# A lambda layer behind a group norm: key maximum on TensorE, group statistics on GpSimd, twelve image buffers, two pairs as plain sums

## The chip, the core and the metric

The kernel runs on one core of a Trainium2 chip. The core has five engines that run beside each other and are joined by semaphores: TensorE (PE, matmuls into PSUM), VectorE (DVE), ScalarE (ACT), GpSimd (POOL) and SyncE (SP, which here issues all transfers). The metric is the time of one execution on the device, in microseconds (us); the median of three runs of the kernel before is 1595.41 us (1594.87 to 1595.89).

## The reference

Cut to what is computed (b = 32 images, d = 128 channels, n = m = 1024 positions, k = 16, h = 4 heads, v = 32):

```
xg = group_norm(x, 32 groups of 4 channels)          # per image
xf = xg.reshape(b, n, d)                              # 1024 rows of 128
keys    = xf @ Wk.T          ; softmax over the 1024 positions
values  = batch_norm(xf @ Wv.T)                       # per position, over images and v
queries = batch_norm(xf @ Wq.T)                       # per k, over everything else
content_lambda   = einsum('bmk,bmv->bkv', softmax_keys, values)
position_lambdas = einsum('nmk,bmv->bnkv', E, values) # E is (1024, 1024, 16): the large product
out = x + einsum('bknh,bkv->bhvn', queries, content_lambda)
        + einsum('bknh,bnkv->bhvn', queries, position_lambdas)
```

## The kernel before

All is float32. A large product is made of two roundings: a matrix is split by ScalarE into a high part (type fp32r, `e_hi`, `v_hi`) and by VectorE into what is left (`e_lo`, `b_lo`, `t_lo`), and three matmuls (hi by hi, lo by hi, hi by lo) are summed.

**Projection stage.** The 32 images come one by one into eight buffers `x_in` (4 KB for each of 128 partitions), in nine batches: two of 2 images, seven of 4. For a batch VectorE takes `BN_STATS` of each half image and combines them (`gn_moments`), TensorE averages over the groups of 4 partitions (`gn_average`), VectorE and ScalarE make scale and shift (`gn_finish`, `gn_sqrt`, a square root on ScalarE), and GpSimd normalises the images in place (`norm_images`, L398). TensorE then transposes an image (L909, 8 matmuls) and projects the one before it (L919), and ScalarE reads both out of PSUM, into `x_t`, and into `v_nat`, `keys`, `q_nat`. After eight images (an octave `a`, four in all) the softmax's maximum is made: VectorE takes it within a partition (`keys_max`), and GpSimd over the partitions by `partition_all_reduce` and subtracts it (`shift_keys`, L403 and L405). `between` says behind which batch VectorE does the statistics of an octave.

**Stage between.** VectorE makes the values' statistics, both engines normalise the values, TensorE makes the content lambdas (64 matmuls, L950) and their sums; differences of value blocks (`t_raw`) are made and everything is split in two parts.

**The pairs.** E is read in 64 pairs of two tiles of 8 rows. With its two halves of positions and the two halves of the images a pair is a 2 by 2 block product. It is made by seven products (`product`, i = 0 to 6, L989) of 4 x 3 matmuls of 128x512, with sums of E's blocks made by GpSimd (`e_sums`, `e_last_sum`) and differences of the values' blocks; banks a, b and c of PSUM are read out between the products by VectorE into `pos` (`evacuate_...`). The pair's lambdas are then multiplied by the queries (`query`, 32 matmuls, L1008), which stands behind product 0 of the next pair; GpSimd spreads the queries for it over `q_diag` (`diag`), and VectorE adds the result to the image (`add_out`).

Every engine runs its list in the order that is written out by hand, so an instruction that waits holds all behind it.

## Time and profile before

| what | value |
|---|---|
| median of three runs | 1595.41 us |
| the profiled execution's own time | 1599.93 us |
| its span (first to last instruction) | 1598.2 us |
| mean TensorE clock granted | 0.968 of full |
| TensorE busy (matmul) | 1483.3 us, 93% |
| VectorE busy | 1016.7 us, 64% |
| GpSimd busy | 675.6 us, 42% |
| ScalarE busy | 427.5 us, 27% |

The slices of the span show where TensorE isn't busy: the first six of forty read 6, 7, 6, 5, 3, 6 tenths, the last 7, and all 33 between them 8 or 9. A busy share says nothing of a wait that comes once; the stretch before the even part is read by stage.

### The profile page before, as it was taken

To read this page: it belongs to the slowest core of one execution; us is meant where nothing else is said; L and a number is where in the kernel's file an instruction comes from. 1 tells how busy PE (TensorE), PEld (TensorE's weight loads), DVE (VectorE), ACT (ScalarE), POOL (GpSimd) and SP (SyncE) were. 2 spreads that over 40 slices of the span, in tenths; PEclk is the share of its full clock that TensorE was granted. 3 is DMA by queue.
4 is the path that set the end of the run, shared out by engine and by line. 5 is a ranking of instruction groups with operands and counts; after the bars stand their busy time and mean duration, and the time that the engine had idled before them with its cause. 6 is when DMAs were issued, how large, how long until landed. Compare 5 with 4: busy or idle time off the path is not lost.

```text
span 1598.2 us, 27819 instructions
## 1 busy us (share of the span) xinstructions
PE 1483.3 (93%) x10407; PEld 1243.3 (78%) x10407; DVE 1016.7 (64%) x1496; ACT 427.5 (27%) x738; POOL 675.6 (42%) x453
## 2 busy tenths in 40 slices
PE   6765368999999999999999999999999999999997
PEld 6655247888888888888888888888888888888886
DVE  6645597666666666666666666666666666666663
ACT  4435432222222222222222222222222222222220
POOL 4333525444444444444444444444444444444441
PEclk9878689999999999999999999999999999999999
DMA  6453142233343434241525243333434251525221
GB/s 227 170 192 112 15 65 60 60 90 68 74 85 85 85 85 86 60 92 45 112 59 112 59 103 67 78 67 85 85 85 85 76 95 47 92 58 112 59 52 27
DMA packets 338460, 134.68 MB, mean 84 GB/s; under 512 B 202640, under 2 KB 333824, under 8 KB 337920
## 3 DMA queue, kind: packets, MB, share of 16 engines
q1 hardware_dynamic: 338432, 134.31, 36.7%
q8 instruction: 17, 0.28, 0.1%
q14 instruction: 11, 0.09, 0.0%
HBM read 109.12 MB, written 25.17 MB: 84 GB/s over the span
## 4 chain that ended last, share of the span: by engine, by line
PE 87%; issue 5%; DVE 3%; POOL 3%; ACT 1%; DMA 0%; DVEq 0%; SPq 0%; POOLq 0%; ACTq 0%
PE ps_a L989 76%; PE ps_b L1008 8%; PE ps_b L919 2%; POOL x_in L398 1%; PE ps_a L909 1%; POOL keys L405 1%; DVE e_lo L679 1%; POOL key_top L403 0%; DVE b_lo L691 0%; DVE bn L639 0%; PE ps_b L950 0%; DVE q_stats L671 0%; DMA x_in<-in_x 0%; DVE t_lo L691 0%; ACT x_t L500 0%
## 5 line engine op out<-in xcount | busy, mean ns | idle before, releaser
L989 PE MATMUL ps_a<-v_hi,e_hi 128*128 128x512 f32 x1792 | 706.0, 394 | 12.8 <-issue 12.1
L989 PE MATMUL ps_a<-v_hi,e_lo 128*128 128x512 f32 x1792 | 699.0, 390 | 0.0
L989 PEld LDWEIGHTS ps_a<-v_hi,e_hi 128*128 128x128 f32 x1792 | 337.1, 188 | 86.6 <-issue 12.9
L989 PE MATMUL ps_a<-b_lo,e_hi 128*128 128x512 f32 x1024 | 399.2, 390 | 2.6 <-DVE b_lo L691 2.6
L989 PEld LDWEIGHTS ps_a<-v_hi,e_lo 128*128 128x128 f32 x1792 | 337.3, 188 | 68.2
L525 ACT ACTIVATE e_hi<-e_nat 128x512 fp32r<-128x512 f32 x320 | 202.1, 632 | 603.4 <-PE ps_a L989 598.3
L437 POOL TENSOR_TENSOR q_diag<-qn,row_mask 128x1024 f32<-128x1024 f32 x128 | 249.1, 1967 | 222.4 <-PE ps_b L1008 208.2
L433 POOL TENSOR_TENSOR e_nat<-e_nat,s_buf 128x512 f32<-128x512 f32 x64 | 83.5, 1305 | 553.3 <-DVE e_lo L679 553.3
L679 DVE TENSOR_TENSOR e_lo<-e_nat,e_hi 128x512 fp32r<-128x512 f32 x320 | 301.1, 941 | 2.0 <-ACT e_hi L525 0.3
L989 PE MATMUL ps_a<-t_lo,e_hi 128*128 128x512 f32 x768 | 300.0, 391 | 0.0
L752 DVE TENSOR_TENSOR pos<-ps_a,content 128x512 f32<-128x512 f32 x189 | 130.7, 692 | 178.4 <-PE ps_a L989 175.9
L989 PEld LDWEIGHTS ps_a<-b_lo,e_hi 128*128 128x128 f32 x1024 | 192.5, 188 | 43.4 <-DVE b_lo L691 3.5
L790 DVE TENSOR_TENSOR res<-ps_b,res 32x512 f32 (+1 forms) x256 | 175.9, 687 | 57.7 <-PE ps_b L1008 55.0
L525 ACT ACTIVATE e_hi<-s_buf 128x512 fp32r<-128x512 f32 x128 | 80.8, 633 | 401.4 <-PE ps_a L989 401.4
L679 DVE TENSOR_TENSOR e_lo<-s_buf,e_hi 128x512 fp32r<-128x512 f32 x128 | 105.2, 822 | 109.7 <-ACT e_hi L525 109.5
L989 PEld LDWEIGHTS ps_a<-t_lo,e_hi 128*128 128x128 f32 x768 | 144.6, 188 | 30.4
L1008 PEld LDWEIGHTS ps_b<-q_diag,pos 128*64 128x64 f32 x4096 | 126.2, 139 | 29.7 <-issue 28.5
L1008 PE MATMUL ps_b<-q_diag,pos 128*64 128x64 f32 x4096 | 135.1, 225 | 7.1 <-DVE pos L854 6.3
L424 POOL TENSOR_TENSOR s_buf<-s_buf,e_nat 128x512 f32<-128x512 f32 x64 | 103.8, 1621 | 5.0
L422 POOL TENSOR_TENSOR s_buf<-e_nat 128x512 f32<-128x512 f32 x64 | 84.0, 1313 | 0.0
L426 POOL TENSOR_TENSOR e_nat<-e_nat 128x512 f32<-128x512 f32 x64 | 83.9, 1310 | 0.0
L779 DVE TENSOR_TENSOR pos<-ps_a,pos 128x512 f32<-128x512 f32 x64 | 44.3, 691 | 54.7 <-PE ps_a L989 54.7
(107 smaller groups left out, 758.5 us busy)
## 6 DMA issues: line engine op xcount, KB each, us to landing
e_nat<-in_L_conv_E SPq DMA_DIRECT2D x128, 512.0 KB, 4.8
x_in<-in_x SPq DMA_DIRECT2D x32, 512.0 KB, 4.2
res<-in_x SPq DMA_DIRECT2D x64, 256.0 KB, 6.8
out_dram<-res SPq DMA_DIRECT2D x64, 256.0 KB, 4.9
q_dram<-q_nat SPq DMA_DIRECT2D x4, 2048.0 KB, 7.6
q_blk<-q_dram SPq DMA_DIRECT2D x32, 256.0 KB, 5.4
gam_q<-in_L_conv_gamma_q SPq DMA_DIRECT2D x8, 0.1 KB, 4.9
bet_q<-in_L_conv_beta_q SPq DMA_DIRECT2D x8, 0.1 KB, 4.6
```

The source lines that it names most:

```text
L422: pool.tensor_tensor(s_buf[:, 0], e_block(slot, 1, 0), e_block(slot, 1, 1), ALU.add).then_inc(s_ready, 1)
L424: pool.tensor_tensor(s_buf[:, 1], s_buf[:, 0], e_block(slot, 0, 0), ALU.subtract).then_inc(s_ready, 1)
L426: pool.tensor_tensor(a21, e_block(slot, 0, 0), a21, ALU.subtract).then_inc(s_ready, 1)
L433: pool.tensor_tensor(a12, a12, s_buf[:, 1], ALU.subtract).then_inc(s_ready, 1)
L437: pool.tensor_tensor(q_diag[:, slot].rearrange("p (q n) -> p q n", n=TN), qn[:, slot].unsqueeze(2).to_broadcast([P, BH, TN]), row_mask[:]. ...
L525: nc.scalar.activation(e_hi[:, i], e_source(i, slot), ACT.Copy).then_inc(e_hi_ready, 1)
L679: nc.vector.tensor_tensor(e_lo[:, i], e_source(i, slot), e_hi[:, i].bitcast(f32), ALU.subtract).then_inc(e_lo_ready, 1)
L752: nc.vector.tensor_tensor(to, bank_a, content[:, cols], ALU.add).then_inc(evacuated, 1)
L779: nc.vector.tensor_tensor(pos[:, 0, right], bank_b, pos[:, 0, right], ALU.add).then_inc(evacuated, 1)
L790: ins = nc.vector.tensor_tensor(r, s, r, ALU.add)
L989: ins = nc.tensor.matmul(BANK_OF[i], e[:, i, j].rearrange("p n k -> p (n k)"), v[:, j], start=(STARTS[i] and j == 0 and n == 0), stop=(STO ...
L1008: ins = nc.tensor.matmul(to, pos[:, t, cols], q_diag[:, t, cols], start=True, stop=True)
```

## The change

1. **Key maximum.** `partition_all_reduce` goes. TensorE transposes `key_max` (`turn_key_max`), VectorE takes the maximum along the free dimension and scales a unit matrix by it (`keys_top`), TensorE multiplies by a matrix of ones, which spreads it to all partitions (`spread_key_top`), VectorE copies it to SBUF (`copy_key_top`), GpSimd subtracts. For the last octave VectorE subtracts, out of PSUM. These use the PSUM columns of one projection buffer, so TensorE's next projection waits for the copy.
2. **Group statistics.** VectorE no longer combines the statistics: the raw sets are squared by one operation, averaged by TensorE, copied, and nine small operations on GpSimd, each waiting for the one before, make scale and shift; the inverse root is `pow` with -0.5 on GpSimd, here and for the values and the queries. ScalarE has no more square roots.
3. **Twelve buffers** for the images instead of eight; `gn_average` of a batch stands one image earlier in each four, and VectorE takes a batch's raw statistics ahead of the octave's work.
4. **Two pairs as plain sums.** Pairs 0 and 1 need no block sums: eight block products (96 matmuls a pair instead of 84) into four banks, with the hi parts straight from ScalarE. Those of pair 0's first half of positions stand ahead of the content lambdas. Their reading out adds `content` at once. What GpSimd did between (`v_nat` difference) VectorE does now.

The core of the diff:

```
-            def gn_sqrt(k):
-                act.wait_ge(gn_var_ready, k + 1)
-                nc.scalar.activation(gn_std[:, slots(k)], gn_var[:, slots(k)], ACT.Sqrt, bias=eps_t[:]).then_inc(gn_std_ready, 1)
             def norm_images(k):
-                pool.wait_ge(gn_ready, k + 1)
+                pool.wait_ge(gn_read, k + 1)
+                link(pool.tensor_tensor(gn_half[:, sl], gn_out[:, sl, 0], gn_out[:, sl, 1], ALU.add))
...
+                link(pool.tensor_tensor(gn_rstd[:, sl], gn_var[:, sl], minus_half[:, sl], ALU.pow))
+                link(pool.tensor_tensor(gn_bias[:, sl], gn_tot[:, sl, 1], gn_rstd[:, sl], ALU.mult))
+                link(pool.tensor_scalar(gn_bias[:, sl], gn_bias[:, sl], -1.0, 0.0, ALU.mult, ALU.add))
             def shift_keys(a):
-                pool.wait_ge(key_max_ready, a + 1)
-                link(pool.partition_all_reduce(key_top[:].rearrange("p g k -> p (g k)"),
-                                               key_max[:].rearrange("p g k -> p (g k)"), P, RMAX))
+                pool.wait_ge(key_spread_ready, a + 1)
+            def turn_key_max(a, reads):
+                pe.wait_ge(key_max_ready, a + 1)
+                pe.wait_ge(proj_read, reads)
+                nc.tensor.transpose(turned_ps, key_max[:].rearrange("p g k -> p (g k)"), ident[:]).then_inc(key_max_turned, 1)
+            def spread_key_top(a):
+                pe.wait_ge(ones_ready, 1)
+                pe.wait_ge(key_diag_ready, a + 1)
+                nc.tensor.matmul(spread_ps, ones_sq[:], key_diag[:], start=True, stop=True).then_inc(key_top_spread, 1)
+            def plain_sums(p, j, passes, last=False):
+                half, slots_of = j // MJ, FIRST_SLOTS[p]
+                for at, (tile, col, bank) in enumerate(((1, 1, bank_d), (1, 0, bank_c), (0, 0, bank_a), (0, 1, bank_b))):
...
+                    if p == 1 and j == 0:
+                        pe.wait_ge(evacuated, (4, 5, 6, 7)[at])
+                    for n, (e, v) in enumerate(((e_hi, hi), (e_lo, hi), (e_hi, lo))):
+                        if n in passes:
+                            ins = nc.tensor.matmul(bank, e[:, slot, j % MJ].rearrange("p n k -> p (n k)"), v,
+...
+            for j in range(MJ):
+                pe.wait_ge(v_hi_ready, j + 1)
+                plain_sums(0, j, (0, 1))
+            lambda_half(0)
+            lambda_half(1)
+            sum_lambdas()
...
+            for j in range(MJ, J - 1):
+                plain_sums(1, j, (0, 1, 2))
+            query(0, first=True)
+            plain_sums(1, J - 1, (0, 1, 2), last=True)
```

Not shown: the same `pow` in `values_rstd` and `queries_rstd`, and what follows from pairs 0 and 1 being plain in the lists of the engines.

On GpSimd, at the batch of images 12 to 15 and the first octave's maximum, before (`key_top` is the reduced maximum, `keys` the projected keys):

```order
L398 TENSOR_SCALAR x_in<-x_in,gn_rstd,gn_bias 128x1024 [waits gn_ready]
L398 TENSOR_SCALAR x_in<-x_in,gn_rstd,gn_bias 128x1024 x3
L403 ISA
L403 ISA key_top<-key_max 128x128 [waits key_max_ready]
L405 ISA
L405 TENSOR_TENSOR keys<-keys,key_top 128x64x16 [waits pool_step]
```

and now, one batch later:

```order
L418 TENSOR_TENSOR gn_half<-gn_out 128x24 [waits gn_read]
L419 TENSOR_TENSOR gn_tot<-gn_half 128x12 [waits pool_step]
L420 TENSOR_TENSOR gn_sq<-gn_tot 128x4 [waits pool_step]
L421 TENSOR_SCALAR gn_var<-gn_tot 128x4 [waits pool_step]
L422 TENSOR_TENSOR gn_var<-gn_var,gn_tot 128x4 [waits pool_step]
L423 TENSOR_TENSOR gn_var<-gn_var,gn_sq 128x4 [waits pool_step]
L424 TENSOR_TENSOR gn_rstd<-gn_var,minus_half 128x4 [waits pool_step]
L425 TENSOR_TENSOR gn_bias<-gn_tot,gn_rstd 128x4 [waits pool_step]
L426 TENSOR_SCALAR gn_bias<-gn_bias 128x4 [waits pool_step]
L429 TENSOR_SCALAR x_main<-x_main,gn_rstd,gn_bias 128x1024 [waits pool_step]
L429 TENSOR_SCALAR x_main<-x_main,gn_rstd,gn_bias 128x1024 x3
L434 TENSOR_TENSOR keys<-keys,key_spread 128x64x16 [waits key_spread_ready]
```

The reduce and the ISA instructions around it are gone, and nine small operations stand ahead of each batch's images.

On TensorE, from the last projection on, before:

```order
L919 MATMUL ps_b<-w_cols,x_t 128x112 x16
L950 MATMUL ps_b<-v_nat,keys 64x128 x64
L957 MATMUL ps_a<-ones,exp_sum 128x1 x4
L989 MATMUL ps_a<-v_hi,e_hi 128x512
L989 MATMUL ps_a<-v_hi,e_lo 128x512
```

and now (with the waits; of the 32 matmuls of L1080 the first two stand):

```order
L996 MATMUL ps_b<-ident,key_max 128x128 [waits proj_read,key_max_ready]
L1001 MATMUL ps_b<-key_diag,ones_sq 128x128 [waits key_diag_ready,ones_ready]
L1080 MATMUL ps_a<-v_hi,e_hi 128x512 [waits v_hi_ready,e_lo_ready]
L1080 MATMUL ps_a<-v_hi,e_lo 128x512
...
L1037 MATMUL ps_b<-v_nat,keys 64x128 [waits v_normed,keys_exp]
```

Thirty-two matmuls of pair 0 moved ahead of the content lambdas.

On VectorE, among the products of pair 0 (`t_lo`, `b_lo` lo parts of the values' differences, `q_stats` the queries' statistics, `pos` and `head` the lambdas, `res` the output), before:

```order
L746 COPY head<-ps_a 128x512 [waits product_done]
L679 TENSOR_TENSOR e_lo<-e_nat,e_hi 128x512 [waits e_hi_ready]
L691 TENSOR_TENSOR b_lo<-v_nat,v_hi 128x4x512 [waits v_hi_ready]
L754 COPY pos<-ps_a 128x512 [waits product_done]
...
L691 TENSOR_TENSOR b_lo<-v_nat,v_hi 128x4x512 [waits lam_half,v_hi_ready]
L679 TENSOR_TENSOR e_lo<-e_nat,e_hi 128x512 [waits e_hi_ready]
L691 TENSOR_TENSOR t_lo<-t_raw,v_hi 128x2048 [waits v_hi_ready]
```

and now, from the first evacuations of pair 0 to its query result:

```order
L805 TENSOR_TENSOR pos<-ps_a,content 128x512 [waits first_summed] x3
...
L720 TENSOR_TENSOR t_lo<-t_raw,v_hi 128x2048 [waits t_hi_ready]
L720 TENSOR_TENSOR b_lo<-v_nat,v_hi 128x4x512 [waits t_hi_ready]
L720 TENSOR_TENSOR t_lo<-t_raw,v_hi 128x2048 [waits t_hi_ready]
L705 TENSOR_TENSOR e_lo<-e_nat,e_hi 128x512 [waits e_hi_ready]
L705 TENSOR_TENSOR e_lo<-s_buf,e_hi 128x512 [waits e_hi_ready] x2
L805 TENSOR_TENSOR pos<-ps_a,content 128x512 [waits queried,first_summed]
L805 TENSOR_TENSOR pos<-ps_a,content 128x512 [waits first_summed] x3
L705 TENSOR_TENSOR e_lo<-e_nat,e_hi 128x512 [waits e_hi_ready] x3
L817 TENSOR_TENSOR res<-ps_b,res 32x32x16 [waits queried,res_loaded]
```

The lo parts of the differences, which before stood between the products of pair 0 (L691), now stand behind the queries' statistics, ahead of pair 2's first splits and of `res`.

## Rows read from the trace of the kernel before

**Rows 1.** Stages: length, busy PE, PEld, DVE, ACT, POOL, PE's clock, DMA share, GB/s.
```profile
11.28:146.20 134.92, 101.73 (x784) 98.78 (x784) 79.39 (x227) 68.20 (x136) 50.96 (x41) 0.86 0.47 163
146.20:269.33 123.13, 61.85 (x393) 50.43 (x393) 86.55 (x139) 40.06 (x49) 51.91 (x31) 0.76 0.29 58
269.33:1598.20 1328.87, 1318.79 (x9229) 1093.39 (x9228) 844.61 (x1113) 317.15 (x549) 569.05 (x365) 1.00 0.36 77
```
**Rows 2.** Chain that ended last: start, us, what; two of the even pairs.
```profile
356.53 19.27 PE ps_a L989 x84
377.81 19.27 PE ps_a L989 x84
```
**Rows 3.** Waits before 269 us: who waited for what, us in total, times, longest.
```profile
POOL keys L405 <- issue: 32.6, 4, 10.3
POOL key_top L403 <- issue: 26.8, 4, 7.8
PE ps_a L909 <- POOL x_in L398: 25.2, 7, 11.8
```
**Rows 4.** TensorE in order of time: start, length, instruction, idle before it.
```profile
26.45 1.04 PE L909 MATMUL ps_a<-ident,x_in 128*128 128x128 f32 x8
27.33 1.94 PE L919 MATMUL ps_b<-w_cols,x_t 128*128 128x112 f32 x16
...
39.84 2.04 PE L919 MATMUL ps_b<-w_cols,x_t 128*128 128x112 f32 x16 [1.17 <-ACT x_t L500]
...
142.44 3.72 PE L919 MATMUL ps_b<-w_cols,x_t 128*128 128x112 f32 x32
...
185.25 8.88 PE L950 MATMUL ps_b<-v_nat,keys 128*64 128x128 f32 x128 [39.09 <-ACT keys L515]
...
246.34 3.69 PE L1008 MATMUL ps_b<-q_diag,pos 128*64 128x64 f32 x64 [6.28 <-DVE pos L854]
...
269.33 2.08 PE L1008 MATMUL ps_b<-q_diag,pos 128*64 128x64 f32 x64
```
**Rows 5.** GpSimd in order of time.
```profile
1.20 0.10 POOL L379 MEMSET eps_t<- 128x1 f32 x1
46.30 5.44 POOL L398 TENSOR_SCALAR x_in<-x_in,gn_rstd,gn_bias 128x1024 f32<-128x1024 f32 x4 [7.88 <-DVE gn_bias L658]
...
139.93 0.46 POOL L415 TENSOR_TENSOR exp_sum<-level 128x128 f32<-128x128 f32 x1
140.35 1.27 POOL L422 TENSOR_TENSOR s_buf<-e_nat 128x512 f32<-128x512 f32 x1
...
190.78 6.69 POOL L461 TENSOR_TENSOR v_nat<-v_nat 128x2048 f32<-128x2048 f32 x1 [0.47 <-issue]
234.51 4.32 POOL L437 TENSOR_TENSOR q_diag<-qn,row_mask 128x1024 f32<-128x1024 f32 x2 [14.18 <-ACT qn L590]
```
**Rows 6.** The line of the reduce: queue's instructions, count, ns.
```profile
L403 POOLq MODIFY_POOL_CONFIG  x8: 8/11/22, 51.7 to 164.0; - x8
```
**Rows 7.** VectorE in order of time.
```profile
33.50 4.84 DVE L639 BATCH_NORM_STATS2 bn<-x_in 128x6 f32<-128x512 f32 x8
59.24 5.31 DVE L671 BATCH_NORM_STATS2 q_stats<-q_nat 128x6 f32<-128x256 f32 x16
164.64 4.43 DVE L723 TENSOR_SCALAR v_nat<-v_nat,v_scale,v_shift 128x1024 f32<-128x1024 f32 x6
192.96 6.66 DVE L735 TENSOR_TENSOR t_raw<-v_nat,t_raw 128x2048 f32<-128x2048 f32 x1
200.14 2.28 DVE L691 TENSOR_TENSOR t_lo<-t_raw,v_hi 128x2048 fp32r<-128x2048 f32 x1
205.35 3.02 DVE L803 SCALAR_TENSOR_TENSOR lam_diag<-ps_b,inv_sum,row_mask 64x128 f32<-64x128 f32 x8
226.57 2.08 DVE L812 BATCH_NORM_AGGREGATE q_mv<-q_stats 128x2 f32<-128x24 f32 x16
235.31 1.70 DVE L679 TENSOR_TENSOR e_lo<-e_nat,e_hi 128x512 fp32r<-128x512 f32 x1 [0.26 <-ACT e_hi L525]
```

More of the change, by code:

```diff
@@ new lines, in _ @@
+            first_lo(0, 3)
+            for j in range(MJ):
+                dve.wait_ge(v_hi_ready, j + 1)
+                nc.vector.tensor_scalar(v_nat[:, j], v_nat[:, j], v_scale[:, j:j + 1], v_shift[:, j:j + 1],
+                                        ALU.mult, ALU.add).then_inc(v_normed, 1)
+            dve.wait_ge(v_normed, MJ)
+            link(nc.vector.tensor_tensor(t_raw[:, 0], raw_block(v_nat, 0, 1), raw_block(v_nat, 0, 0), ALU.subtract))
+            some_query_stats(2, range(4, KD)).then_inc(q_stats_done, 1)
@@ L847, in _ @@
-            evacuate_c21(0, with_content=False)
-            for n in range(NP - 1):
-                split_lo(1, n, 1)
-            evacuate_c12(0)
-            dve.wait_ge(content_ready, 1)
-            dve.wait_ge(evacuated, NP)
-            for t in range(2):
-                nc.vector.tensor_tensor(pos[:, t], pos[:, t], content[:], ALU.add).then_inc(content_added, 1)
+            t_split_lo(2, 2)
+            t_split_lo(3, 3)
+            t_split_lo(5, 4)
+            split_lo(2, 0, 0)
+            split_lo(2, 1, 0)
@@ L856, in pair @@
+            split_lo(2, 2, 0)
+            evacuate_first(1)
+            for n in range(3, NP - 1):
+                split_lo(2, n, 0)
+            add_out(0, new_block=True)
             def pair(p, i, second, last):
@@ L877, in pair @@
                     split_lo(p + 1, 5, (i + 1) % 2)
-            for i in range(1, PPB):
-                pair(i, i, i == 1, False)
+            for i in range(2, PPB):
+                pair(i, i, i == 2, False)
             with dve.Fori(1, BLOCKS - 1) as blk:
@@ L938, in _ @@
+                    if i % GB == 1 and b < B - GB:
+                        gn_average(b // GB + 2, b - 1)
             project(B - 1, G - 1)
[L940 to L954 removed]
@@ L955, in _, with lambda_half @@
-            pe.wait_ge(exp_summed, A)
-            for s in range(B // TN):
-                ins = nc.tensor.matmul(sum_ps[:, s:s + 1], exp_sum[:, s * P:(s + 1) * P], ones[:], start=True, stop=True)
-            ins.then_inc(lam_summed, 1)
+            turn_key_max(A - 1, B)
+            spread_key_top(A - 1)
+            def lambda_half(half):
+                if half == 0:
+                    pe.wait_ge(keys_exp, A)
+                for j in range(half * MJ, half * MJ + MJ):
+                    if j < MJ:
+                        pe.wait_ge(v_normed, j + 1)
+                    else:
+                        pe.wait_ge(v_normed_act, j - MJ + 1)
+                    for s in range(B // TN):
+                        for h in range(2):
+                            g = 2 * s + h
+                            ins = nc.tensor.matmul(ps_b[h * HALF:(h + 1) * HALF, s // 2, (s % 2) * BANK:(s % 2) * BANK + P],
+                                                   keys[:, j, g].rearrange("p a k -> p (a k)"), v_nat[:, j, g * P:(g + 1) * P],
+                                                   start=(j == 0), stop=(j == J - 1))
+                ins.then_inc(lam_half, 1)
@@ L960, in spread_content, with sum_lambdas @@
+            def sum_lambdas():
+                pe.wait_ge(exp_summed, A)
+                for s in range(B // TN):
+                    ins = nc.tensor.matmul(sum_ps[:, s:s + 1], exp_sum[:, s * P:(s + 1) * P], ones[:], start=True, stop=True)
+                ins.then_inc(lam_summed, 1)
             def spread_content():
@@ L997, in query @@
                 pe.wait_ge(q_diag_ready, p * 2 + 2)
[L998 to L1000 removed]
+                if not first:
                     pe.wait_ge(res_added, p)
```

604 lines of the change are left out of this document (329 added, 275 removed).

## The prediction

> **What bounds the kernel now.** I read the stages first [rows 1]. From 269.33 us on TensorE is busy for 1318.8 of 1328.9 us at its full clock, and the chain of waits runs there through its matmuls alone, a pair every 21.28 us [rows 2]. Nothing in that stretch is changed: query 1, which opens it, still stands behind product 0 of pair 2, and pairs 2 to 63 keep their products. So the change is worth what it moves the start of query 1, at 269.33 [rows 4]. Ahead of it lie two stages that TensorE doesn't bound: 134.9 us of projections (101.7 busy) and 123.1 us up to query 1 (61.9 busy) [rows 1].
>
> The projection stage: at full clock an image costs TensorE 0.88 us of transposes (26.45 to 27.33) and 1.78 of projections (3.72 less 1.94), 2.66 together [rows 4], 85 for 32. The other 50 are stalls, and the waits name them: before each of the four reduces GpSimd sits 26.8 us in sum with nothing shown that it waits for, and behind them, before the subtraction, another 32.6; two of the four hold back the next images, so TensorE waits 25.2 us for normalised images [rows 3], and it runs at a mean clock of 0.86 [rows 1]. The other two reduces follow the projections: the content lambdas wait 39.09 us for the last octave's keys [rows 4].
>
> **Reduce out, TensorE in.** The four reduces and 59.4 us of unexplained wait around them go. In their place stand, in the first three octaves, a transpose and a ones matmul (128 columns each; the eight transposes of an image take 0.88 us, so 0.1 to 0.4 each) and a round trip: VectorE's maximum and scaling (0.4), the matmul, its copy behind two `BN_STATS` of 0.6 [rows 7]. TensorE's projection waits behind it on its queue, and ScalarE's reads behind that: I take 0.9 us of wait and 0.4 of work an octave, 4 for three. Less than 0 isn't possible (work is added); 3 an octave would be the whole trip uncovered.
>
> The Trainium skill (GPSIMD Engine Reference, Engine selection) gives a reduction along partitions to GpSimd and elementwise work to VectorE; this change does the reverse of both. The rows decide against it here: a reduce comes with 59.4 / 4 = 14.9 us of idle GpSimd, against under 2 us by TensorE [rows 3, 4]. By that rule the sum would have to lose, not gain.
>
> **Small operations on GpSimd.** Nine per batch, each waiting for the one before, in nine batches. No row shows an operation on 2 to 24 columns, nor a `pow`. Below, a memset of one column takes 0.10 us; above, a `TENSOR_TENSOR` of 128 columns 0.46, and one of 512 1.27 [rows 5], a slope of 2.1 ns a column and so some 0.19 us with no columns. I take 0.2, with 0.07 for the wait between (139.93 plus 0.46 is 140.39, little over where the next begins), and 0.5 for the `pow`: 9 x 0.27 + 0.3 = 2.7 us a batch. A `pow` I bound by 0.10 below and by 1.27 above, the nearest two-input rows. With 4.8 us for four images (5.44 when VectorE works beside it) [rows 5] GpSimd needs 7.5 to 8.2 us of the 10.6 that TensorE takes for four: hidden, save in the first batch, where the chain replaces a shorter one on VectorE and ScalarE. That is 1.5 us: the first transposes start at 12.8 instead of 11.3. VectorE gains what it loses of the combining (32 aggregates and five small operations a batch), and ScalarE no longer changes its table in this stage.
>
> **Twelve buffers and the order.** With `gn_average` an image earlier and VectorE's raw statistics ahead of the octave's work, the statistics are late only where sixteen query statistics (5.31 us [rows 7]) stand in front of the copy: 2 us, twice. The start, where the third batch's four images take 4.84 us of statistics [rows 7], stalls 3.2 us as before. Once an octave ScalarE's two `x_t` in a row cost TensorE 1.35 (1.17 in [rows 4]): 4 for three. The loads run at 163 GB/s in this stage with store traffic in it [rows 1]; 16.8 MB over 103 us is the same rate, so they don't become the bound, and with four more buffers they are issued earlier. A last 2 us: single waits for images and the last read.
> Sum: 12.8 + 85 + 4 + 4 + 3.2 + 4 + 2 = 115. The last projection ends at 115, not 146.2 (142.44 + 3.72 [rows 4]): 31 us.
>
> **From the last projection to query 1.** TensorE's own work: 192 plain matmuls and 12 of pair 2 at 19.27 + 2.02 less its query, 19.05 for 84 or 0.227 each [rows 2], is 46.3; content lambdas 8.9 [rows 4], and some 5 for sums, spreading and query 0: 60. That is 24 matmuls (5.4 us) more than before, and they don't set the end, because VectorE has more. In its order, with durations from [rows 7]: 8 value statistics of half the columns 1.6 (0.33 at 256, 0.6 at 512), their aggregates 1.1, the maximum 2.4, scale and shift 0.8, the transposed maximum 0.4, subtraction 1.2, first split 0.6, four normalisations 3.0, `t_raw` 2.2, twenty query statistics 6.6, two lo parts 4.4, the diagonal 3.1, three differences 6.6, two lo parts 4.4, four splits 2.5, four evacuations 2.6, eight query statistics 2.6, moments 2.9, four lo parts of differences 8.8, the queries' affine 1.5, six splits 3.8, four evacuations 2.6, `res` 2.8. Sum 68.5. It starts 0.5 us behind the last projection.
> To this come waits. For semaphores 4 (the spread maximum, the first sums, the queries' mean, the root on GpSimd). And for GpSimd: in this stretch it has four `q_diag` of 1.95 and four or more sums of 1.3, next to nine splits of VectorE that read two SBUF tensors. Where such two meet, one stands still: `t_raw` took 6.66 us beside GpSimd's 6.69 us of `v_nat`, and 2.28 is what its kind takes alone; a split took 1.70 beside `q_diag` [rows 5, 7] instead of 0.6. I take 12, all of GpSimd's 13 but one. Sum: 0.5 + 68.5 + 4 + 12 = 85. Before, this stage took 123.1 [rows 1]: 38 us less, of which the 39 us wait is the most; and 115 + 85 = 200.
>
> The Trainium skill (SBUF — State Buffer, Who interferes with whom) calls the port pair of VectorE and GpSimd an exclusive lock, held for a whole instruction. By that rule the pair's waits are 12 as taken; by bandwidth shared between them they would be near 0 and the sum 188. The 6.66 agrees with the lock (4.4 of wait and 2.2 of work).
>
> TensorE has gaps of some 7 and 2 us just ahead of query 1, where before it ran evenly. Query 0, behind a gap of 6.28 us, took 3.69 us instead of 2.08 [rows 4]: I add 2.5 for the lower of the clock's two levels (those 1.6, and half of it again for products beside it), and nothing is taken back later.
> Query 1 then starts at 202.5, 66.8 earlier: a span of 1598.2 - 66.8 = 1531.4, an own time of 1599.93 - 66.8 = 1533.1. The profiled execution lies 4.5 above the median of the runs, so the median becomes 1595.4 - 66.8 = 1528.6.
>
> **Rivals.**
> A. The tail is shorter: VectorE and GpSimd meet less (the waits of 12 fall to 2, and with shorter gaps the 2.5 us of clock go). For it: operations with PSUM in them, evacuations and `res`, are not slowed in the even part. Against: `t_lo` and the splits aren't of that kind. 1529 - 12 = 1517.
> B. GpSimd becomes the bound of the projection stage. At 0.46 a small operation, the upper row, a batch costs 9 x 0.53 + 5.4 = 10.2, and with a subtraction of 2.3 and a sum of 2.5 an octave 22.8 to 25.2 against TensorE's 21.3: 8 batches at about 2 us more, 16: 1545. For it: dispatch dominates such operations and the floor of 0.19 is from a slope.
> C. Slower. The reduce's line has eight `MODIFY_POOL_CONFIG` [rows 6], two for each of four uses, and 14.9 us of idle time around each use. If `pow` too is code that GpSimd must fetch and put back, each of nine batches in the stage and two uses behind pays 14.9: 11 x 14.9 = 164, less a slack of 2.5 us in eight batches, 144: 1529 + 144 = 1673. It decides from about (67 + 20) / 11 = 8 us a use. Against it: the changed program has no such pair of instructions around `pow`, as it had around the reduce.
> The Trainium skill (GPSIMD Engine Reference, Instruction dispatch) puts about 6 us on the first call of a freshly loaded kernel, unseen in the profile. The 6.7 us ahead of each reduce (26.8 / 4) agree; whether `pow` is resident no row tells.
> D. The change doesn't do what it says in the first octaves: the round trip through VectorE holds TensorE as the reduce held GpSimd (VectorE is busy 79 of 135 us, more with the smaller stage), and half of the 25 us comes back: 1541.
>
> **How the numbers follow.** Forecast 1529 with its own range 1521 to 1537: 0.50. A 0.18, B 0.15, D 0.09, C 0.04; 0.04 for what I don't see, spread on both sides. A to the forecast and up to B is held by 1512 to 1548, and C with part of the rest is left out. 0.2%, 3.2 us, is about what a measurement of this kernel tells from no change. Faster 0.95, same 0.01, slower 0.04: only C and half of the unseen lie there.
>
> **What would show it.** After the change: no gap over 4 us between transposes from 20 to 110 us, and a last projection ending within 5 us of 115; GpSimd's small operations at 0.2 and its batch under 9 us (B: over 10; C: gaps of 6 us beside L424). From there VectorE busy for over 80% and TensorE not, query 1 at 202, with waits of VectorE for GpSimd in `t_lo`, `b_lo` and the splits (A: none). The pairs after it at 21.28 us: were they slower, the remainder isn't the same, and the prediction is wrong from its first step.

## The result and the profile after

The changed kernel took 1536.49 us (median of 4 runs, 1534.77 to 1536.83), the one before 1595.65 (4 runs): a ratio of 0.9626, 95% interval 0.9609 to 0.9642, 59 us less. The prediction said 1529, its own range 1521 to 1537, so the result lies inside by 0.5 us. The profiled execution took 1534.77 us, its span is 1533.0; forecast were 1533.1 and 1531.4.

Stages of the changed kernel: from the first image's transposes to the last projection, from there to query 1, and the rest (start and end, then length, busy PE, PEld, DVE, ACT, POOL, PE's clock, DMA share, GB/s), and below them one of its even pairs, and the start of the next, in the chain that ended last.

```profile
12.76:116.70 103.94, 92.19 (x793) 89.33 (x793) 72.29 (x152) 66.11 (x130) 69.04 (x110) 1.00 0.63 206
116.70:204.28 87.58, 66.92 (x420) 54.49 (x420) 78.06 (x139) 34.78 (x40) 33.00 (x23) 0.88 0.41 82
204.28:1533.00 1328.72, 1318.83 (x9228) 1093.40 (x9228) 848.19 (x1114) 317.56 (x549) 573.01 (x367) 1.00 0.37 77
```

```profile
247.11 2.02 PE ps_b L1113 x64
249.13 19.26 PE ps_a L1096 x84
268.39 2.02 PE ps_b L1113 x64
```

The remainder is the one before, 1328.72 us against 1328.87 [rows 1], and a pair still takes 21.28 (247.11 to 268.39) [rows 2]. All of the gain lies ahead of query 1. The projections now end at 116.70 (146.2 before) at full clock, the stage behind them takes 87.58 us (123.1 before), and in it VectorE is busy for 89%, TensorE for 76%.

TensorE in order of time, the rows that answer to [rows 4]: first transposes, last projections, query 0, the first product and query 1.

```profile
12.76 1.94 PE L979 MATMUL ps_a<-ident,x_main 128*128 128x128 f32 x8 [4.74 <-POOL x_main L429]
...
112.87 3.83 PE L989 MATMUL ps_b<-w_cols,x_t 128*128 128x112 f32 x32 [0.38 <-DVE key_spread L742]
...
188.24 2.08 PE L1113 MATMUL ps_b<-q_diag,pos 128*64 128x64 f32 x64 [1.87 <-POOL q_diag L475]
199.17 0.77 PE L1096 MATMUL ps_a<-v_hi,e_hi 128*128 128x512 f32 x1 [5.90 <-DVE pos L805]
204.28 2.09 PE L1113 MATMUL ps_b<-q_diag,pos 128*64 128x64 f32 x64
```

What TensorE waited for up to 117 us (who for what, us in total, times, longest):

```profile
PE ps_a L979 <- POOL x_main L429: 5.1, 2, 4.7
PE ps_b L989 <- ACT x_t L531: 3.5, 3, 1.2
PE ps_b L971 <- DVE bn L679: 3.2, 2, 2.6
PE ps_b L989 <- issue: 3.2, 2, 1.6
PE ps_b L989 <- DVE key_spread L742: 2.0, 3, 0.8
```

The 25.2 us for normalised images [rows 3] are 5.1, of which 4.7 are the start. The round trips of the maximum cost 2.0 in three.

One batch on GpSimd, and TensorE's average ahead of it and the batch's first image behind it:

```profile
31.64 0.33 PE L971 MATMUL ps_b<-bn,group_avg 128*128 128x48 f32 x2
37.12 1.04 PE L979 MATMUL ps_a<-ident,x_more 128*128 128x128 f32 x8
```

```profile
32.30 0.23 POOL L418 TENSOR_TENSOR gn_half<-gn_out 128x24 f32<-128x24 f32 x1 [2.50 <-DVE gn_out L684]
32.61 0.21 POOL L419 TENSOR_TENSOR gn_tot<-gn_half 128x12 f32<-128x12 f32 x1
...
34.04 1.02 POOL L424 TENSOR_TENSOR gn_rstd<-gn_var,minus_half 128x4 f32<-128x4 f32 x1
...
35.73 4.77 POOL L429 TENSOR_SCALAR x_more<-x_more,gn_rstd,gn_bias 128x1024 f32<-128x1024 f32 x4
```

A small operation takes 0.20 us and 0.08 pass between two; `pow` takes 1.02 on 4 columns. The chain is 3.43 us (32.30 to 35.73), its first image is ready at about 35.73 + 4.77 / 4 = 36.92, and TensorE takes it at 37.12: 0.20 us of slack. Worked out in the same way it is 0.2, 0.2, 1.8, 0.1 and 1.8 us in the fourth to eighth batch, and in the ninth TensorE waits 0.37 us. The two batches with 1.8 are those in which a round trip of the maximum stands between the average and the batch's first image.

VectorE and GpSimd in the last stretch before query 1:

```profile
112.73 5.12 DVE L710 TENSOR_TENSOR e_lo<-e_nat,e_hi 128x512 fp32r<-128x512 f32 x3
173.71 2.28 DVE L720 TENSOR_TENSOR t_lo<-t_raw,v_hi 128x2048 fp32r<-128x2048 f32 x1
182.86 3.42 DVE L720 TENSOR_TENSOR b_lo<-v_nat,v_hi 128x2048 fp32r<-128x2048 f32 x1 [0.56 <-ACT v_hi L583]
186.20 4.04 DVE L720 TENSOR_TENSOR t_lo<-t_raw,v_hi 128x2048 fp32r<-128x2048 f32 x1
```

```profile
112.90 2.74 POOL L434 TENSOR_TENSOR keys<-keys,key_spread 128x1024 f32<-128x1024 f32 x1 [6.41 <-DVE key_spread L742]
180.77 7.32 POOL L475 TENSOR_TENSOR q_diag<-qn,row_mask 128x1024 f32<-128x1024 f32 x2 [1.26 <-ACT qn L616]
188.06 3.34 POOL L460 TENSOR_TENSOR s_buf<-e_nat 128x512 f32<-128x512 f32 x1
```

A `t_lo` of one size took 2.28 us alone and 4.04 beside `q_diag` and the sum of E behind it (`s_buf`); the two `q_diag` took 7.32 instead of 4.32 [rows 5].

### The profile page after: what moved, and what is told of

Same layout as the page of the kernel before. It is cut to its first block, busy times and chain, and to the rows that moved or that the text cites. A ratio compares the mean times of both kernels' runs of the same rounds, so it can differ in the third digit from the quotient of the medians.

```text
span 1533.0 us, 28096 instructions
## 1 busy us (share of the span) xinstructions
PE 1478.9 (96%) x10443; PEld 1237.9 (81%) x10443; DVE 1004.7 (66%) x1416; ACT 420.0 (27%) x721; POOL 681.2 (44%) x524
## 4 chain that ended last, share of the span: by engine, by line
PE 92%; DVE 5%; POOL 2%; issue 1%; ACT 0%; DMA 0%; DVEq 0%; SPq 0%; POOLq 0%; ACTq 0%
PE ps_a L1096 78%; PE ps_b L1113 8%; PE ps_b L989 3%; PE ps_a L979 1%; PE ps_a L1080 1%; DVE bn L676 1%; DVE q_stats L697 1%; POOL q_diag L475 0%; DVE e_lo L710 0%; DMA x_main<-in_x 0%; DVE v_nat L882 0%; DVE bn L679 0%; POOL s_buf L460 0%; DVE v_stats L691 0%; DVE pos L805 0%
## 5 line engine op out<-in xcount | busy, mean ns | idle before, releaser
L1096 PE MATMUL ps_a<-v_hi,e_hi 128*128 128x512 f32 x1736 | 683.1, 393 | 6.1 <-DVE pos L805 5.9
L1096 PE MATMUL ps_a<-v_hi,e_lo 128*128 128x512 f32 x1736 | 676.7, 390 | 0.0
L1096 PEld LDWEIGHTS ps_a<-v_hi,e_hi 128*128 128x128 f32 x1736 | 326.4, 188 | 76.5 <-issue 6.6
L1096 PE MATMUL ps_a<-b_lo,e_hi 128*128 128x512 f32 x992 | 386.5, 390 | 0.0
L1096 PEld LDWEIGHTS ps_a<-v_hi,e_lo 128*128 128x128 f32 x1736 | 326.6, 188 | 66.1
L569 ACT ACTIVATE e_hi<-e_nat 128x512 fp32r<-128x512 f32 x310 | 196.2, 633 | 595.2 <-PE ps_a L1096 588.5
L475 POOL TENSOR_TENSOR q_diag<-qn,row_mask 128x1024 f32<-128x1024 f32 x128 | 254.4, 2009 | 206.2 <-PE ps_b L1113 205.0
L705 DVE TENSOR_TENSOR e_lo<-e_nat,e_hi 128x512 fp32r<-128x512 f32 x310 | 295.1, 952 | 0.3
L1096 PE MATMUL ps_a<-t_lo,e_hi 128*128 128x512 f32 x744 | 290.2, 390 | 0.0
L1096 PEld LDWEIGHTS ps_a<-b_lo,e_hi 128*128 128x128 f32 x992 | 186.7, 188 | 38.8
```

The lines of the kernel that those rows point to most:

```text
L475: pool.tensor_tensor(q_diag[:, slot].rearrange("p (q n) -> p q n", n=TN), qn[:, slot].unsqueeze(2).to_broadcast([P, BH, TN]), row_mask[:]. ...
L569: nc.scalar.activation(e_hi[:, i], e_source(i, slot), ACT.Copy).then_inc(e_hi_ready, 1)
L705: nc.vector.tensor_tensor(e_lo[:, i], e_source(i, slot), e_hi[:, i].bitcast(f32), ALU.subtract).then_inc(e_lo_ready, 1)
L1096: ins = nc.tensor.matmul(BANK_OF[i], e[:, i, j].rearrange("p n k -> p (n k)"), v[:, j], start=(STARTS[i] and j == 0 and n == 0), stop=(STO ...
```

## The experiments

Each was compared with the kernel before on its chip: runs 1 to 4, 5 to 8 and 9 to 12 shared a chip each, and there the kernel before took 1595.8, 1595.8 and 1598.4 us. "End" is the end of the last projection, "query 1" its start, both in the profiled execution; in the changed kernel they are 116.7 and 204.3.

| run | median, us | ratio to before, 95% | span | end | query 1 |
|---|---|---|---|---|---|
| changed kernel | 1536.49 | 0.9626 (0.9609 to 0.9642) | 1533.0 | 116.7 | 204.3 |
| 1 reduces back | 1571.55 | 0.9844 (0.9827 to 0.9861) | 1569.0 | 139.5 | 240.2 |
| 2 maximum alone | 1563.35 | 0.9790 (0.9773 to 0.9808) | 1561.5 | 125.8 | 234.0 |
| 3 eight buffers | 1548.44 | 0.9701 (0.9683 to 0.9720) | 1546.8 | 130.4 | 218.1 |
| 4 finish on VectorE | 1538.90 | 0.9644 (0.9625 to 0.9663) | 1536.7 | 122.1 | 209.6 |
| 5 lambdas first | 1541.73 | 0.9657 (0.9638 to 0.9677) | 1537.7 | 116.4 | 208.9 |
| 6 eight more operations | 1551.27 | 0.9711 (0.9692 to 0.9731) | 1551.9 | 135.3 | 223.2 |
| 7 twenty-four more | 1601.40 | 1.0028 (1.0018 to 1.0039) | 1601.4 | 185.1 | 272.8 |
| 8 sums early | 1535.29 | 0.9620 (0.9598 to 0.9641) | 1531.3 | 116.6 | 202.4 |
| 9 changed kernel again | 1537.28 | 0.9616 (0.9603 to 0.9630) | 1535.6 | 119.2 | 206.8 |
| 10 gap filled | 1530.31 | 0.9578 (0.9565 to 0.9592) | 1528.6 | 118.6 | 199.8 |
| 11 mean taken early | 1529.33 | 0.9563 (0.9550 to 0.9577) | 1528.0 | 120.3 | 199.2 |
| 12 as 6, average early | 1550.59 | 0.9697 (0.9682 to 0.9713) | 1549.4 | 133.1 | 220.6 |

**1. The reduces back.**

```
-                pool.wait_ge(key_spread_ready, a + 1)
+                pool.wait_ge(key_max_ready, a + 1)
+                link(pool.partition_all_reduce(key_spread[:].rearrange("p g k -> p (g k)"),
+                                               key_max[:].rearrange("p g k -> p (g k)"), P, RMAX))
...
-                        spread_key_top(a - 1)
-                        pe.wait_ge(key_spread_ready, a)
...
-                        turn_key_max(a - 1, b - 1)
```

> The changed kernel with all four reduces over partitions back on GpSimd, one batch later than in the kernel before, and everything else of the change kept. Theory (a reduce costs about 15 us of idle GpSimd wherever it stands): the two inside the projection stage cost 15 less 2.3 of slack a batch, some 12 each, and the two behind it delay the last keys by 10 to 15: a span of 1533.0 + 24 + 12 = 1569, range 1560 to 1580. Rival (the twelve buffers give the images a lead that covers the reduce, and the gain came from the other parts): below 1542.

36.0 us more in the span, 34 to 35 in the medians, as expected (22.8 up to the last projection, 13.1 behind). But not by the way expected; that the sum came out is luck. The waits up to 145 us:

```profile
PE ps_b L984 <- ACT x_t L535: 26.5, 5, 11.5
ACT keys L550 <- POOL keys L437: 26.3, 3, 12.1
POOL keys L437 <- issue: 21.4, 3, 7.7
POOL key_spread L435 <- issue: 18.3, 3, 6.5
...
PE ps_a L974 <- POOL x_main L430: 7.0, 2, 4.7
```

The reduce has its 6.5 and 7.7 us again, but images are late by only 2 us more than in the changed kernel (7.0 against 5.1). ScalarE waits for the shifted keys with its exponential, its reads of TensorE's transposes stand behind, and TensorE waits for these 26.5 us instead of 3.5: the 23 us that the stage is longer. The buffers and the later place do cover the reduce for the images, as the rival had it; the cost went through ScalarE's queue. Whether a later exponential would take it away wasn't tried.

**2. The maximum by TensorE alone**, in the kernel before.

```
-                pool.wait_ge(key_max_ready, a + 1)
-                link(pool.partition_all_reduce(key_top[:].rearrange("p g k -> p (g k)"),
-                                               key_max[:].rearrange("p g k -> p (g k)"), P, RMAX))
+                pool.wait_ge(key_spread_ready, a + 1)
...
                 gn_moments(k)
+                if k in (5, 7):
+                    keys_top((k - 5) // 2)
                 gn_finish(k)
+                if k in (5, 7):
+                    copy_key_top((k - 5) // 2)
...
+                    if i == 7 and a > 0:
+                        spread_key_top(a - 1)
+                        pe.wait_ge(key_spread_ready, a)
...
+                    if i == 6 and a > 0:
+                        turn_key_max(a - 1, b - 1)
```

> The kernel before with the key maximum by TensorE alone: eight buffers, group statistics on VectorE and ScalarE, block products from pair 0 on. Theory: 25.2 us of waits for normalised images go less 4 for the round trips, and of the 39.09 us wait for the last keys some 13 go, since the values are normalised at 169 and the content lambdas started at 185: a span of 1598.2 - 21 - 13 = 1564, range 1556 to 1574; the other parts then have the remaining 31. Rival 1 (the maximum is nearly the whole gain): 1545 or less. Rival 2 (VectorE's round trip through TensorE holds the images in this order): above 1580.

Confirmed: the projections end 20.4 us earlier than before (21 expected), query 1 comes 35.3 earlier (34 expected). The other three parts bring the remaining 26 us (1563.35 to 1537.28). From this run's trace to the changed kernel's, query 1 comes 29.7 us earlier, 9.1 of it in the projection stage and 20.6 behind it.

**3. Eight buffers.**

```
-    SLOTS = 3 * GB
+    SLOTS = 2 * GB
...
-            return x_main[:, s] if s < MAIN else x_more[:, s - MAIN]
+            return x_main[:, s]
```

> The changed kernel with eight image buffers instead of twelve, order of the instructions unchanged. Theory: VectorE takes a batch's raw statistics one batch ahead, and with eight buffers the last two images of that batch are loaded only after two more images are transposed, so VectorE waits some 8 us in its queue and all behind it is late: 3 us a batch in six batches, a span of 1551, range 1543 to 1562. Rival (loads are at 163 to 206 GB/s and are never late): 1533 to 1535.

12 us more, inside the range, all in the projection stage (13.7). The waits show the cause: VectorE waits for the images' loads, 22.2 us against 0.7 in the changed kernel.

```profile
DVE bn L673 <- DMA x_main<-in_x: 22.2, 12, 5.5
```

**4. Scale and shift on VectorE and ScalarE.** The first six of the small operations are the same on VectorE, behind its copy, and the places of the square roots in ScalarE's list (not shown) come back.

```
                 sl = slots(k)
-                pool.wait_ge(gn_read, k + 1)
-                link(pool.tensor_tensor(gn_half[:, sl], gn_out[:, sl, 0], gn_out[:, sl, 1], ALU.add))
...
+                pool.wait_ge(gn_ready, k + 1)
...
+                link(nc.vector.tensor_tensor(gn_half[:, sl], gn_out[:, sl, 0], gn_out[:, sl, 1], ALU.add))
...
+                dve.wait_ge(gn_std_ready, k + 1)
+                link(nc.vector.reciprocal(gn_rstd[:, sl], gn_std[:, sl]))
+                nc.vector.scalar_tensor_tensor(gn_bias[:, sl], gn_tot[:, sl, 1], -1.0, gn_rstd[:, sl],
+                                               ALU.mult, ALU.mult).then_inc(gn_ready, 1)
...
+            def gn_sqrt(k):
+                act.wait_ge(gn_var_ready, k + 1)
+                nc.scalar.activation(gn_std[:, slots(k)], gn_var[:, slots(k)], ACT.Sqrt).then_inc(gn_std_ready, 1)
```

> The changed kernel with scale and shift of the group norm made by VectorE with a square root by ScalarE, as in the kernel before, instead of nine small operations on GpSimd. Theory: some 2 us more of VectorE and two changes of ScalarE's function table a batch; VectorE has 32 us free in the projection stage and ScalarE 38, so half of it is covered: a span of 1543, range 1537 to 1552. Rival (the place of the small operations is indifferent, all is hidden): 1531 to 1535, or below by 2 from the first batches.

The medians differ by 2.4 us from the changed kernel's first comparison and by 1.6 from its second, and the intervals of the ratios overlap: of the time alone it can't be said that this part does anything. The projections ended at 122.1 here and at 116.7 and 119.2 there. The span, 1536.7, lies between the theory's range and the rival's, and 1.1 above that of run 9: nearer to the rival.

**5. Content lambdas ahead of the plain sums.**

```
+            lambda_half(0)
+            lambda_half(1)
+            sum_lambdas()
             pe.wait_ge(e_lo_ready, 2)
             for j in range(MJ):
                 pe.wait_ge(v_hi_ready, j + 1)
                 plain_sums(0, j, (0, 1))
-            lambda_half(0)
-            lambda_half(1)
-            sum_lambdas()
```

> The changed kernel with the 32 matmuls of pair 0's first half of positions behind the content lambdas and their sums instead of ahead of them. Theory (TensorE doesn't set the end of this stretch, VectorE does): they start about 6 us later than the lambdas do now, VectorE's first evacuations wait some 4 us longer, and its diagonal can't start earlier because VectorE comes to it at 147 anyway: a span of 1533 to 1538. Rival (TensorE's order is on the path, every us of it counts): 7 to 10 more, 1541 or above.

Between the two in size: 4.6 us at query 1 (5.2 and 4.5 in the medians). TensorE waits in three places for the normalised values, and what follows the lambdas on it is 5.0 us late (L1053 at 165.33 instead of 160.31). VectorE's diagonal starts at 147.5 as in the changed kernel (147.9), and then it waits:

```profile
170.34 2.48 DVE L805 TENSOR_TENSOR pos<-ps_a,content 128x512 f32<-128x512 f32 x4 [5.97 <-PE ps_a L1080]
```

In the changed kernel this wait is 1.05 us. It grew by 4.9, and query 1 came 4.6 later: from the first evacuations on every us of TensorE counted, as the rival has it, and my theory that TensorE doesn't set the end fell. In the changed kernel too VectorE waits for TensorE here, so TensorE has no slack at this point.

**6, 7 and 12. More small operations, and an earlier average.**

```
+                for _ in range(8):       # 24 in run 7
+                    link(pool.tensor_scalar(gn_sq[:, sl], gn_bias[:, sl], -1.0, 0.0, ALU.mult, ALU.add))
                 for i in range(sl.start, sl.stop):
                     xi = x_in(i)
```

and in run 12 besides:

```
-                    if i % GB == 1 and b < B - GB:
+                    if b == 1 or (i % GB == 0 and GB <= b < B - GB):
                         gn_average(b // GB + 2, b - 1)
```

Not shown of run 12: the averages from the fourth batch on have PSUM columns of their own, and the projection that waits for VectorE's copy of one (`gn_read`) is one earlier as well.

> The changed kernel with eight more operations on 2 to 4 columns, each waiting for the one before, in each of the nine batches on GpSimd: 8 x 0.28 = 2.2 us a batch. Theory (the chain is hidden behind TensorE's 10.6 us a batch from the third batch on, and lies on the path in the first one or two): 2.2 to 5 more, a span of 1535 to 1538. Rival B (GpSimd bounds the projection stage): 9 x 2.2 = 20 more, 1553.

> As the one with eight more operations, but with twenty-four: 24 x 0.28 = 6.7 us a batch, which then takes 15 us on GpSimd against 10.6 on TensorE. Both theories have GpSimd as the bound here; they differ by the slack: with 2.3 us of it a batch, 6.7 to 12 for the start and 7 x 4.4 = 31 behind it, a span of 1571 to 1577; without slack 9 x 6.7 = 60, 1593.

> The changed kernel with eight more small operations a batch on GpSimd (as in the run that lasted 1551.3 us), and the averages of the statistics from the fourth batch on put one image (2.66 us) earlier in TensorE's list. Theory (what counts is the time from a batch's average on TensorE to its first normalised image, 5.1 us against the 5.3 that two images give; GpSimd itself is idle 2 to 5 us before each batch): 2.2 us in each of the first three batches and little in the other six, with 2 to 4 for VectorE's copies that come late once an octave: a span of 1542, range 1539 to 1546. Rival (GpSimd's throughput bounds the stage): 1548 to 1552 as before.

My theory for run 6 fell: 18.6 us more up to the last projection (14.8 in the medians; the profiled execution was the longest of its four), where 9 x 2.24 = 20.2 were added, and a span of 1551.9 where rival B had 1553. Run 7: 68 us (64.9 in the medians) for 9 x 6.7 = 60. That the totals are near what was added doesn't mean that each batch pays for what it got. The stages of runs 6 and 7, as above:

```profile
15.74:135.29 119.55, 99.49 (x793) 96.05 (x793) 71.50 (x152) 66.33 (x130) 82.94 (x174) 0.94 0.51 167
19.27:185.05 165.78, 112.90 (x793) 109.48 (x793) 66.35 (x152) 66.30 (x130) 106.91 (x302) 0.82 0.34 115
```

Of run 6's 18.6 us, 3.0 are a later start and 12.0 more waits for images behind it; 7.3 are more busy time of TensorE (99.5 against 92.2), at a granted clock of 0.94 instead of 1.00; and 3.7 of other waits are gone. The sixth and the eighth batch, which had 1.8 us of slack, wait only 0.32 each. So where there was slack it hid the chain, and what wasn't hidden cost a wait and then a slower TensorE.

Nor is GpSimd busy; run 6, GpSimd ahead of three batches:

```profile
54.78 0.23 POOL L418 TENSOR_TENSOR gn_half<-gn_out 128x24 f32<-128x24 f32 x1 [5.59 <-DVE gn_out L686]
69.34 0.23 POOL L418 TENSOR_TENSOR gn_half<-gn_out 128x24 f32<-128x24 f32 x1 [3.57 <-DVE gn_out L686]
84.02 0.23 POOL L418 TENSOR_TENSOR gn_half<-gn_out 128x24 f32<-128x24 f32 x1 [1.95 <-DVE gn_out L686]
```

Ahead of the third batch and of the ninth GpSimd has no such gap. It is a loop: the average stands in TensorE's list two images ahead of the batch it serves, and two images last 5.5 us, while average, copy, chain and first image take 5.3 (31.64 to 37.12 and to 36.92 in the changed kernel). What is added to the chain comes out of a slack of 0.2, or 1.8 in two batches. Run 12 tests this. TensorE waiting for images, first the last such row of run 12, then four of run 6, the first of them with the projection behind it:

```profile
31.78 1.48 PE L982 MATMUL ps_a<-ident,x_main 128*128 128x128 f32 x8 [2.46 <-POOL x_main L432]
```

```profile
45.69 1.71 PE L981 MATMUL ps_a<-ident,x_more 128*128 128x128 f32 x8 [1.93 <-POOL x_more L431]
47.19 3.00 PE L991 MATMUL ps_b<-w_cols,x_t 128*128 128x112 f32 x16
...
61.68 1.10 PE L981 MATMUL ps_a<-ident,x_main 128*128 128x128 f32 x8 [1.92 <-POOL x_main L431]
90.93 1.09 PE L981 MATMUL ps_a<-ident,x_more 128*128 128x128 f32 x8 [2.24 <-POOL x_more L431]
119.92 1.09 PE L981 MATMUL ps_a<-ident,x_main 128*128 128x128 f32 x8 [3.62 <-POOL x_main L431]
```

From the fourth batch on, where the average is earlier, run 12 has no such wait, and run 6 has 10.4 us of them, with the same work on GpSimd: for these waits the loop is shown as the cause, and not GpSimd's throughput. The total doesn't show it: 1550.59 us lies in the rival's range and not in mine, and the last projection ends only 2.2 us earlier than in run 6 (by the ratios too it is 2 us). Other waits took the place, 2 to 4 us by my expectation and 11 in fact: 3 more for VectorE's raw statistics, and 8 for its copy of the average, which now stands behind sixteen query statistics.

```profile
77.79 3.73 PE L994 MATMUL ps_b<-w_cols,x_t 128*128 128x112 f32 x16 [4.07 <-issue]
110.37 3.73 PE L994 MATMUL ps_b<-w_cols,x_t 128*128 128x112 f32 x16 [4.06 <-issue]
```

```profile
72.27 5.31 DVE L700 BATCH_NORM_STATS2 q_stats<-q_nat 128x6 f32<-128x256 f32 x16
77.50 0.18 DVE L687 COPY gn_out<-ps_b 128x48 f32<-128x48 f32 x1
```

**8. Sums of E early.**

```
             sum_keys(3)
+            e_sums(2, 0, 64, first=True)
             queries_rstd()
...
             diags(0)
-            e_sums(2, 0, 64, first=True)
```

> The changed kernel with GpSimd's three sums of E for pair 2 ahead of the root of the queries' variance, in the stretch in which it is idle (133 to 179 us), instead of behind the first two spread queries, where they took 6.2 us on the chain that ended last and met VectorE's last lo parts. Theory: the chain through the spread queries loses those 6 us and VectorE its waits for them (3 to 4), so query 1 starts 5 us earlier: a span of 1528, range 1526 to 1530. Rival 1 (VectorE's work sets the end and the sums merely meet other two-input work of VectorE at 135 to 145): 1531 to 1534. Rival 2 (their new place holds the last keys' sums or the value differences): above 1534.

Query 1 came 1.9 us earlier, and the times can't be told from the changed kernel's. The span, 1531.3, is rival 1's. The sums' 6 us are gone from GpSimd's queue, and the spread queries of pair 1 moved into their place, onto VectorE's next splits:

```profile
190.57 4.81 DVE L705 TENSOR_TENSOR e_lo<-s_buf,e_hi 128x512 fp32r<-128x512 f32 x2
```

```profile
190.21 4.63 POOL L475 TENSOR_TENSOR q_diag<-qn,row_mask 128x1024 f32<-128x1024 f32 x2 [2.31 <-PE ps_b L1113]
```

Two splits take 1.3 alone (run 11, below). The collision was moved, not removed.

**9. The changed kernel again.**

> The changed kernel once more, unedited, beside the two that follow. If the single profiled execution of the kernel before (1599.93 us) was an unusually long one of its kind, the difference of medians is some 6 us smaller than the 66.8 that was worked out from it: 59 us, ratio 0.963. If instead the chip of the first comparison was at fault, the ratio is 0.959.

The first: ratio 0.9616, and 0.959 lies outside its interval. The difference is 61 us (1598.4 less 1537.3), not 66.8. More under the term from the profile to the median below.

**10 and 11. A gap of VectorE filled, and the queries' mean earlier.** Run 10 is run 8 with the first edit, run 11 has both.

```
-            some_query_stats(2, range(4))
+            some_query_stats(2, range(KD)).then_inc(q_stats_done, 1)
+            first_lo(0, 0)
+            first_lo(0, 1)
             keys_top(2)
...
-            for n in range(3):
-                first_lo(0, n)
+            first_lo(0, 2)
...
-            some_query_stats(2, range(4, KD)).then_inc(q_stats_done, 1)
```

```
             for j in range(MJ):
                 ins = plain_sums(1, j, (0, 1, 2))
+                if j == 1:
+                    average_queries()
             ins.then_inc(half_done, 1)
-            average_queries()
```

> The kernel with early sums of E, and besides that twelve query statistics (4.0 us) and two lo parts of E (1.3 us alone, 3.4 where they met GpSimd's subtraction) moved on VectorE into the 8.1 us in which it waits for the turned key maximum. Theory (VectorE's work sets the end of the last stretch): its work behind the last projection falls by 4.0 + 2.1 us, query 1 starts 6 us earlier than the 202.4 of the kernel with early sums: a span of 1525.5, range 1524 to 1529. Rival (TensorE, which runs without a gap from 127.6 to 188, has become the bound): only its own start moves, by 2 us: 1529 to 1530.

> The same with the queries' mean taken by TensorE behind 24 instead of 48 matmuls of pair 1, since their moments are then ready some 5 us before TensorE comes to it. Theory: the chain scale and shift, spread queries, query 0 moves by up to 5 us, and VectorE's lo parts don't wait: 3 us less than the kernel without this, a span of 1522.5, range 1520 to 1527. Rival (query 0 isn't on the path, the lo parts and evacuations are): equal to the kernel without this within 1 us.

Both beat the changed kernel beside which they ran: 1530.31 and 1529.33 against 1537.28 us, 7.0 and 8.0 less. From the last projection to query 1 it is 87.6 us in the changed kernel (both profiles), 85.9 in run 8, 81.1 in run 10, 78.9 in run 11. Of the 6.1 expected of the filling 4.8 came; VectorE now waits for image 31's values instead:

```profile
119.08 1.64 DVE L691 BATCH_NORM_STATS2 v_stats<-v_nat 128x6 f32<-128x128 f32 x8 [2.15 <-ACT v_nat L536]
```

In run 11 `q_diag` of pair 0 is out of the way before the lo parts, and these have their own length again:

```profile
182.42 2.38 DVE L720 TENSOR_TENSOR b_lo<-v_nat,v_hi 128x2048 fp32r<-128x2048 f32 x1 [3.54 <-ACT v_hi L583]
184.73 2.28 DVE L720 TENSOR_TENSOR t_lo<-t_raw,v_hi 128x2048 fp32r<-128x2048 f32 x1
...
187.53 1.28 DVE L705 TENSOR_TENSOR e_lo<-s_buf,e_hi 128x512 fp32r<-128x512 f32 x2
191.60 2.69 DVE L807 TENSOR_TENSOR pos<-ps_a,content 128x512 f32<-128x512 f32 x4 [2.79 <-PE ps_a L1080]
```

What VectorE no longer loses to GpSimd, it waits for ScalarE (3.54) and TensorE (2.79). In run 11's stretch VectorE is busy for 66.0 and TensorE for 64.7 of 78.9 us, and just ahead of query 1 TensorE waits 2.44 us for VectorE's `res`: neither bounds it alone.

Run 10's span, 1528.6, lies in its range, but nearer to its rival's 1529 to 1530. Run 11 missed its range: 1528.0 where 1520 to 1527 was expected, 0.6 less than run 10, as its rival had it. Behind the last projection it is 2.2 us shorter (3 expected), but its projections ended 1.7 later. In the medians it is 1.0 below run 10; the five times of each don't overlap (1527.87 to 1529.70 and 1530.16 to 1531.86), the intervals of the ratios do.

## Why the prediction was right, and where it was not

**The first step, that only the start of query 1 counts:** right. The remainder was 1328.7 us of 1328.9.

**The projection stage, 115:** 116.7, and term by term: start 12.8 (12.76), round trips 4 (2.0 of wait and some 2 of work), `x_t` 4 (3.5), the third batch's statistics 3.2 "as before" (2.6; in the kernel before the longest wait of this kind was 1.9), late copies twice 2 (twice 1.6), single waits 2 (0.4). All the waits together are 11.7 us where 15.9 were taken, and TensorE's own work is 92.2 where 86.2 were: the averages of the statistics (2.9 us, L971) had no term, and the transposes of the first two images took 1.94 and 1.60 us instead of 1.04. So the sum came nearer than its terms. Taking the reduce out was worth 20.4 us here in the kernel before (run 2) and 22.8 in the changed one (run 1), of the 31 forecast for the stage.

**The stage behind, 85 and 2.5 for the clock:** 87.6. The sum is right, its terms are not, and that is luck in part. VectorE is idle for 9.5 us (87.58 less 78.06) where 0.5 and 4 were taken, and busy for 78.06 where 68.5 and 12 were: 5.0 too little and 2.4 too much, together the 2.6 above 85, which had been put down to the clock. Its waits for GpSimd come to 10.3 where 12 were taken (the first three splits 3.3, most of it ahead of the stage, a diagonal 0.9, the lo parts 1.1 and 1.8, the splits behind them 3.3, each its length less its own); four normalisations took 4.5 where 3.0 were taken, with GpSimd's sums of the keys beside them. The clock's 2.5 came in another place: query 0, which was to take 1.6 of it, took 2.08 us, and product 0 took 5.1 (199.17 to 204.28, granted clock 0.56, behind a wait of 5.90) instead of 2.7. Rival A (those waits near nothing) didn't come: its order is that of run 11, and there other waits took part of the room. The Trainium skill (SBUF — State Buffer, Who interferes with whom) has the shared port as an exclusive lock. Runs 8 and 11 agree as far as they go (4.81 and 1.28 us for the same two splits, with and without `q_diag` beside them).

**The small operations.** The price was right at 0.20 and 0.08, `pow` was 1.02 instead of 0.5, the chain 3.4 instead of 2.7. "Hidden, save in the first batch" held, but for a reason that I had wrong, and so by luck: I compared 7.5 to 8.2 us of GpSimd with 10.6 of TensorE and saw 2.5 us of slack a batch. What had to fit was 5.3 us of latency into two images of 2.7. The slack was 0.2 or less in four of the last six batches and 1.8 in two; rivals B and C were priced with a slack that did not exist, and two more us in each `pow` would have cost 13 to 17 (an estimate by run 6: 14.8 to 18.6 for 2.24 a batch). B came only when eight operations were added. C itself fell: no `pow` took over 1.02 us but the values' of 8 columns (1.79, beside VectorE).

**From the profile to the median.** This term holds most of the miss of 7.9 us. Spans: forecast 1531.4, measured 1533.0, 1.6 off. But I took 66.8 us off the median, though they had been worked out on an execution that lay 4.5 above it, and the changed kernel's profiled execution lay 1.7 below its own median. Of the kernel before, seven runs beside runs 1 to 4 had spans of 1592.9 to 1598.4 with a median of 1594.1, so that profile (1598.2) was at the long end; the changed kernel's (1533.0) was the shortest of its four. Run 9's lies 2.6 higher, and 2.5 of that are in the projection stage (119.2 against 116.7; the stage behind is 87.6 in both): there the third image's transposes and the projection behind them took 1.74 and 2.93 us instead of 1.05 and 1.94 (1.6 us in sum, at a granted clock of 0.60 instead of 1.00), one projection waited 2.80 instead of 1.60 us, and the stage started 0.3 earlier. So the stage that the change shortens is also the one whose length varies from run to run. That the kernel before varies in the same place isn't shown, since there is one profile of it.

**Parts.** Maximum: 32 us alone (run 2), 34 to 35 when undone (run 1). Buffers 12 (run 3). Statistics: 2, not clear of noise (run 4). If parts simply added, some 12 us would be left for the plain pairs and the new order of VectorE, which weren't tried by themselves. That they add isn't shown: with the maximum in place already, the rest brings 20.6 us behind the projections (run 2 against the changed kernel), where the plain pairs and the order act. The Trainium skill (GPSIMD Engine Reference, Engine selection) would have the reduction over partitions on GpSimd; runs 2 and 1 decide against it for this kernel by 32 and 34 us.

## What to carry to other kernels

Throughput is not slack: where an engine serves another in a loop, measure the time from the instruction that starts it to the first one that needs it, and compare it with the place left between the two in the queue, batch by batch. An engine that waits holds what is behind it, so a late result can cost through a third engine (here ScalarE's exponential) while its own user is on time. And a gain worked out on a profile is to be set against other spans of the same kernel before it is taken off a median.
